# Edge stage of a graph network: the penalty of the running maximum spread by TensorE into PSUM

## The reference, cut to what matters

```
d = gelu(LN(gelu(LN(coords @ Wd1 + bd1)) @ Wd2 + bd2))          # per edge
logits  = w1[target] - w2[source] + d
seg_max = segment_max(logits, target)
e       = exp(logits - seg_max[target])
out     = segment_sum(e / segment_sum(e, target)[target] * (w3[source] + d), target)
```

## Time and profile before

| what | value |
| --- | --- |
| median of three runs | 3010.53 us |
| the profiled execution's own time | 2996.25 us |
| its span | 2994.5 us |
| TensorE matmuls busy | 1861.0 us (62%) |
| VectorE busy | 2220.2 us (74%) |
| ScalarE busy | 1823.8 us (61%) |
| GpSimd busy | 996.1 us (33%) |
| mean granted TensorE clock | 0.767 |
| the stage's first and last lg start | 1576.8 and 2673.5 us |

### The profile page before, as it was taken

How to read it: one execution, slowest core, us unless ns; L and a number is a source line. 1 busy time by engine, 2 the same in 40 slices (tenths; PEclk the granted TensorE clock), 3 DMA queues, 4 the chain that set the end, 5 groups by cost and what they waited for, 6 DMA issues and landing times. The chain is left out here.

```text
span 2994.5 us, 39181 instructions
## 1 busy us (share of the span) xinstructions
PE 1861.0 (62%) x7030; PEld 998.4 (33%) x7043; DVE 2220.2 (74%) x4641; ACT 1823.8 (61%) x2345; POOL 996.1 (33%) x985
## 2 busy tenths in 40 slices
PE   3465565478777677458846666666666666640746
PEld 1122222233333222122233444344434444430746
DVE  4799999589999587759827777777777777766434
ACT  0166666468888444359827888787888888860010
POOL 1000000000000010023217777777777777753000
PEclk8679879656676799779957777777777777865868
DMA  2134444225454699336515666666666666650716
GB/s 86 38 134 147 148 148 145 96 74 189 165 195 160 251 370 363 150 132 219 197 40 173 194 202 199 194 199 183 202 197 194 194 191 199 201 156 21 276 58 230
DMA packets 303359, 517.07 MB, mean 173 GB/s; under 512 B 40978, under 2 KB 239458, under 8 KB 290458
## 3 DMA queue, kind: packets, MB, share of 16 engines
q1 hardware_dynamic: 269402, 421.04, 40.5%
q0 software_dynamic: 26720, 54.65, 7.6%
q10 hardware_dynamic: 7200, 40.96, 3.5%
HBM read 282.58 MB, written 236.39 MB: 173 GB/s over the span
## 5 line engine op out<-in xcount | busy, mean ns | idle before, releaser
L1805 POOL DMA_INDIRECT es_got<-w,es_idx x808 | 845.1, 1046 | 341.1 <-issue 332.9
L1941 PE MATMUL en_pv<-en_sq,avg 128*128 128x512 f32 x202 | 183.0, 1003 | 351.2 <-ACT en_sq L2048 351.2
L1402 PE MATMUL acc<-src_hot,dst_hot 128*128 128x401 f16 x1008 | 242.6, 396 | 176.5 <-DVE src_hot L1377 160.3
L1377 DVE TENSOR_SCALAR src_hot<-iota,col_key 128x400 f16<-128x400 f16 x1008 | 316.3, 314 | 0.0
L1375 DVE TENSOR_SCALAR dst_hot<-iota_blk,row_key 128x128 f16<-128x128 f16 x1008 | 247.6, 246 | 11.8 <-PE acc L1402 11.3
L812 PE MATMUL pd_dn<-hT,pd_lhs 66*128 66x512 f32 (+1 forms) x350 | 223.6, 815 | 27.9 <-DVE pd_top L915 22.6
L1402 PEld LDWEIGHTS acc<-src_hot,dst_hot 128*128 128x128 f16 x1008 | 110.2, 109 | 309.2 <-issue 270.8
L2005 DVE TENSOR_TENSOR es_lg<-es_dn,es_w2p 128x512 f32<-128x512 f32 x101 | 69.5, 688 | 190.0 <-PE es_w2p L1897 183.8
L2076 ACT COPY es_rows<-es_rp 128x512 f32<-128x512 f32 x202 | 118.2, 585 | 148.7 <-PE es_rp L1923 146.7
L1068 PE MATMUL ns_acc<-ns_w,ns_val 128*65 128x512 f32 (+1 forms) x350 | 160.0, 609 | 70.6 <-DVE ns_w L1028 70.6
L1431 ACT COPY cbuf<-acc 128x401 f32<-128x401 f32 x200 | 98.4, 492 | 147.9 <-PE acc L1402 114.9
(11 more groups left out here) (499 smaller groups left out, 4684.3 us busy)
## 6 DMA issues: line engine op xcount, KB each, us to landing
rows<-es_rows SPq DMA_DIRECT2D x202, 256.0 KB, 2.7
counts_part<-cbuf SPq DMA_DIRECT2D x50, 800.0 KB, 3.7
near<-pd_out SPq DMA_DIRECT2D x25, 1600.0 KB, 6.2
ns_near<-near SPq DMA_DIRECT2D x25, 1600.0 KB, 9.9
ns_cnt<-counts_part SPq DMA_DIRECT2D x25, 1600.0 KB, 6.7
ss_cnt<-counts_part SPq DMA_DIRECT2D x25, 1600.0 KB, 6.6
n_ct<-turned ACTq DMA_DIRECT2D x50, 800.0 KB, 6.2
lg_plane<-es_lg SPq DMA_DIRECT2D x101, 256.0 KB
```

What stands on the lines that cost most here:

```text
L1377: TS(src_hot[:, s, i, 0:PART].unsqueeze(1), k["iota16"][:, 0:PART].unsqueeze(1), k["col_key"][:, bass.ds(BATCH * b + i, 1)], None, ALU.is_ ...
L1402: last = nc.tensor.matmul(flat[:, bass.ds(places[i], PART + 1)], dst_hot[:, s, i, :], src_hot[:, s, i, 0:PART + 1], start=False, stop=Fals ...
L1805: pool.indirect_dma_start(got[:, s, t, half * 2 * F:(half + 1) * 2 * F], None, d["w23"], bass.IndirectOffsetOnAxis(ap=idx[:, s, half, t:t ...
L1941: nc.tensor.matmul(pv[:, :], avg[:, :], sq[:, :], start=True, stop=True).then_inc(var, 1)
```

## The change

The penalty no longer comes spread over the partitions from DRAM. SP loads the two rows of penalties as they are (es_flags, 2 x 512, one load a step). A constant es_of_half (2 x 128, 1 where the column belongs to the row's half) is made once by VectorE. After the w3 turns TensorE waits for that load and for the step's lg, and multiplies es_of_half with the flags into es_w2p, the bank that held the turned w2 rows which lg has just read. The maximum scan waits for this product (penned) and reads its second operand from that bank, in f32. As the bank is now in use until the scan is done, the w2 turns of the next step wait for max_ready instead of lg_ready.

```diff
-        pen = sb("es_pen", [P, 2, BANK], BF16)
+        flags = sb("es_flags", [2, 2, BANK], BF16)
+        of_half = sb("es_of_half", [2, P], BF16)
...
                 def load_penalty(h, s):
                     c = 2 * h + s
-                    for half in range(2):
-                        sp.dma_start(pen[half * F:(half + 1) * F, s, :],
-                                     d["starts"][half:half + 1, bass.ds(c * BANK + 1, BANK)].to_broadcast([F, BANK]))\
-                          .then_inc(pen_loaded[s], 16)
+                    sp.dma_start(flags[:, s, :], d["starts"][:, bass.ds(c * BANK + 1, BANK)]).then_inc(pen_loaded[s], 16)
...
                 def turn_in(h, s):
                     c = 2 * h + s
                     pe.wait_ge(gathered[s], 16 * 2 * CT * (h + 1))
-                    pe.wait_ge(lg_ready, c)
+                    pe.wait_ge(max_ready, c)
                     for t in range(CT):
                         last = nc.tensor.transpose(w2p[:, t * P:(t + 1) * P], got[:, s, t, 0:4 * F:2], k["ident"][:, :])
                     last.then_inc(turned2, 1)
...
                     last.then_inc(turned3[s], 1)
+                    pe.wait_ge(pen_loaded[s], 16 * h + 16)
+                    pe.wait_ge(lg_ready, c + 1)
+                    nc.tensor.matmul(w2p[:, :], of_half[:, :], flags[:, s, :], start=True, stop=True).then_inc(penned, 1)
...
-                pe.wait_ge(id_made, 1)
+                pe.wait_ge(id_made, 2)
...
                 nc.vector.tensor_copy(id16[:, :], k["ident"][:, :]).then_inc(id_made, 1)
+                nc.vector.tensor_scalar(of_half[:, :], k["half_sel"][:, :], 0.0, None, ALU.not_equal).then_inc(id_made, 1)
...
-                    dve.wait_ge(pen_loaded[s], 32 * h + 32)
                     nc.vector.tensor_copy(mx[:, s, 0:1], mx[:, o, BANK:BANK + 1]).then_inc(carry, 1)
-                    dve.wait_ge(lg_ready, c + 1)
-                    nc.vector.tensor_tensor_scan(mx[:, s, 1:BANK + 1], lg[:, s, :], pen[:, s, :],
+                    dve.wait_ge(penned, c + 1)
+                    nc.vector.tensor_tensor_scan(mx[:, s, 1:BANK + 1], lg[:, s, :], w2p[:, :],
                                                  mx[:, o, BANK:BANK + 1], ALU.max, ALU.add).then_inc(max_ready, 1)
```

More of the change, by code:

```diff
@@ L1765, in edge_softmax @@
                "dec_ready", "e_ready", "ev_ready", "s0_ready", "s1_ready", "rows_turned", "rows_out", "carry", "zeroed",
-               "passed")
+               "passed", "penned")
         (turned2, lg_ready, v3_ready, max_ready, rise, dec_in, e_in,
-         dec_ready, e_ready, ev_ready, s0_ready, s1_ready, rows_turned, rows_out, carry, zeroed, passed) = (
+         dec_ready, e_ready, ev_ready, s0_ready, s1_ready, rows_turned, rows_out, carry, zeroed, passed, penned) = (
              sem(f"es_{x}") for x in one)
```

## The result

The changed kernel took 3258.47 us (median of four runs, 3253.11 to 3262.80) against 3009.15 us before: a ratio of 1.0835, 95% interval 1.0812 to 1.0859. It is 249 us slower; 22 were forecast, and the range ended at 3066.

What follows compares the result with a forecast made beforehand. The edge stage's ring of waits among VectorE, TensorE and ScalarE was taken as the bound, not an engine's busy share. +33 (branch) - 11 (gathers) = +22 us on 3010.53 gave 3033 us, 0.7% slower; range 3001 to 3066.

Steps and rivals of the forecast that it cites:

- I take 0: TensorE's clock: new 0.5 us pause before the penalty matmul and shorter pause before the variance product offset each other, 0 us.
- slow kind: Edge-stage steps of 11.00 us at granted clock 0.66, against 9.99 at 0.84; all steps going there was priced +14 us.
- A clock that moves by over 0.05: Sign that the prediction is wrong: the edge stage's mean granted clock moves by over 0.05 either way.
- The branch's spare time of 0.58: Mean time a step by which ScalarE's row copies finish before VectorE's e; taken to hide 0.58 of 0.85 us delay.
- The branch: Row turns on TensorE, then ScalarE's row copies ahead of e: e 0.33 us later a step, +33 us (bounds +11, +45).
- rival 2: TensorE's clock rises as its long pause before the variance product shrinks: sum -21 us, 2990 us; chance 0.10.
- rival 3: Row-turn branch costs more and TensorE's clock falls: +45 - 5 + 14 = +54 us, 3065 us; chance 0.15.
- The gathers: GpSimd gathers stop being stretched inside the maximum scan, so GpSimd builds a lead over its pauses: -11 us (0 to -14).
- The scan's operand: VectorE's maximum scan reads its second operand as f32 from PSUM: 0 us; the skill's figures would give +6.5 us.
- The scan's wait: VectorE's maximum scan waits for the penalty matmul, at worst 0.1 us late: counted 0, up to +10 if the branch had cover.
- Loads and SP: Two broadcast loads a step become one load of two rows; SP's queue is on no critical chain: 0 us.
- the ring: Edge-stage cycle of waits, VectorE for TensorE, TensorE for ScalarE, ScalarE for both, setting the 10.97 us step.

Runs made afterwards that it cites:

- experiment 5: Changed kernel with the penalty matmul over all 128 array rows, flags and weights zero-padded, same result and columns: 2987.08 us, 0.9940 of the kernel before.
- experiment 11: Kernel before, with the maximum scan reading turned w2 rows in PSUM as second operand; next w2 turns wait for the scan: 2990.78 us, 0.9955.
- experiment 4: Kernel before plus TensorE's wait for lg and a two-row matmul on constant data ahead of the row turns; scan and loads unchanged: 3258.97 us, 1.0855.
- experiment 9: Kernel before plus eight extra 128x128 by 128x512 bf16 matmuls a step ahead of the variance product: 2954.13 us, 0.9819.
- experiment 8: Changed kernel plus eight extra 128x128 by 128x512 bf16 matmuls a step in TensorE's long pause before the variance product: 2948.74 us, 0.9809 of the kernel before.

## Why the prediction was wrong, point by point

**The step that failed is the clock's: "I take 0", with +14 us as the end for "all steps of the slow kind".** The granted clock fell from 0.78 to 0.55, and that cost some 270 us: 3258 against 2987 with the matmul over all rows. A clock that moves by over 0.05 was among the signs that the prediction itself named as wrong. Two things went wrong in it. The new pause of 0.5 us was seen, but weighed against the long pause that got shorter; and the two-row matmul behind it was priced as work, where for the clock it had the effect of idle time, so that the cut in the burst was about 0.75 us (2217.36 to 2218.09) and not what the pause alone makes. The bound was also taken from the wrong rows. The "slow kind" of step had a granted clock of 0.66, still high for a third of the time, and just in the burst. A whole step at the lower level stood nowhere in the trace of before, but its price could have been read from single matmuls there, which were at either level: two 128x512 f32 products in 1.1 or 2.07 us, the four turns in 0.60 or 1.06. An estimate with the stage's means: the row turns start 0.97 us later, they then take 0.15 longer, linear_b 0.64 and the second row turns 0.44, together 2.20 us at ScalarE's second row copy; measured were 2.16 (4.99 us after lg against 2.83, in the steps with all records). The half-clock times are those of the changed kernel's trace, and the trace of before has them too in single cases. The branch's spare time of 0.58 is far from covering that.

**The branch, +33 us: right in place, wrong in size.** The row turns did come later (1.28 us after lg; 1.0 to 1.2 forecast) and ScalarE's wait for VectorE's e did vanish. But with the clock kept (experiment 5) e is only 0.07 us later than before (4.05 after lg against 3.98), although the row turns start 0.80 us later (1.10 against 0.30). The later burst runs at full clock more often: the first row turns take 0.84 us instead of 0.96 and linear_b 1.09 instead of 1.27, so ScalarE's second row copy comes only 0.52 us later (3.35 against 2.83), and the spare time of 0.58 covers most of that. The stretch from e to the next lg fell from 7.00 to 6.78 us, with the clock at 0.81 instead of 0.78. The same shows when only the wait is added: e at 4.06, then 6.73 us to the next lg, and 22 us faster. The sum had treated the durations behind the pause as fixed. So rival 2, "the clock rises", and rival 3, "the clock falls", were both real, on either side of a small edit. Rival 3 gave the fall +14 us where some 270 were measured. That rival 2's 2990 us lies near the 2987 of experiment 5 is luck: it adds a branch of 33 us that did not come and a gain of 43 from the clock that was about half as large.

**The gathers, -11 us: right in size, the reason only in part.** Alone it measured -12.5 us (0.9955, so 7 to 20 us), and the waits for a gather were gone. But the stretch moved on to the next instructions, the mean gather hardly changed, and the lead that GpSimd was to build up by shorter gathers is not shown. In the changed kernel itself the term had nothing to act on: its mean gather is longer than before (1.126 us), and with a step of 13.54 us no w2 turn waits for a gather. The rule of the Trainium skill (SBUF — State Buffer, who interferes with whom) agrees with these traces: a scan with one input in PSUM stretches no gather, the ones with two in SBUF do.

**The scan's operand, 0: right.** 1.27 us with the penalty in PSUM, in the changed kernel as in experiment 11. The 65 ns estimated from the figures of the Trainium skill (VectorE: DVE Perf Modes, the TRN2 errata) for a PSUM source do not show.

**The scan's wait, 0: right.** The scan starts 1.41 us after lg in both kernels, even at half clock; the penalty matmul's 0.60 us ends at 2218.15, just ahead of 2218.22.

**Loads and SP, 0: right** as far as experiment 4 can tell, which leaves them as they were and has the same time within the interval (1.0855 against 1.0835).

## What to carry to other kernels

Before a wait or a thin matmul is put into TensorE's burst, price every matmul behind it at both levels of the clock, and take as the bound the step with the whole burst at the lower one, even if the trace shows no such step. The two-row matmul was short work but no cover for the clock here; padding it with zero rows was worth 271 us and cost TensorE no time that shows (0.39 us against 0.38 at full clock, 0.61 against 0.60 at half). If TensorE is on the ring and its clock is not always full, try useless full-array matmuls in its longest pause first: on the kernel before they gave 1.8% by themselves (experiment 9), while the changed kernel without them gained 0.6% in its best form (experiment 5).

## What the runs showed of the hardware that was not expected

- In this kernel the clock hung on how many rows the penalty matmul uses: the same 512 columns over 2 rows left the stage at 0.55, over 128 rows, 126 of them zeros, at 0.81.
- It changes between two states by little: a pause of about 0.3 us in the burst kept 0.80, and 1.0 us gave 0.58 and 282 us more (2981 and 3263 us). With the long pause filled, 1.2 us between the w3 turns and the row turns left it at 0.97 (experiment 8).
- Eight useless products of 128x512 a step raised it to 0.97. The step was then 10.44 us in experiment 8 and 10.54 in experiment 9; in 1000 us TensorE's waits for a gather were 17 and 29 us.
- A gather of GpSimd that begins inside a scan with both inputs in SBUF is mostly stretched, one inside a scan with an input in PSUM is not (0 of 91). It is not only scans: of 92 gathers that begin during dec = lg - mx, a subtraction with both inputs in SBUF, 91 take over 1.1 us in the changed kernel. If the maximum scan lets a gather pass, a later instruction often catches one.
